# A decoder's self-attention on one NeuronCore: the value products move from the end of each step to its middle

## What is computed

```
x = LN(x + attention0(x))          causal, 16 heads of 16, rotary
x = LN(x + cross_attention(x, ctx))
x = LN(x + routed experts(x))
x = LN(x + attention1(x))          differential: 16 heads x 2 halves of 8, not causal
x = LN(x + latent attention(ctx, x))
x = LN(x + experts that choose tokens(x))

# attention0
scores = einsum('bhqd,bhkd->bhqk', q, k) * scale
scores = where(causal, finfo.min, scores)
attn = softmax(scores);  out = einsum('bhqk,bhkd->bhqd', attn, v)

# attention1
attn1 = softmax(q1 k1^T * scale) v12;  attn2 = softmax(q2 k2^T * scale) v12
a = rms(attn1 - lam * attn2) * rms_weight * (1 - LAMBDA_INIT)
```

## Time and profile before

| | |
|---|---|
| median of 3 runs | 4248.61 us (4227.96 to 4248.86) |
| the profiled execution's own time | 4232.43 us |
| its span, first to last instruction | 4230.7 us |
| PE / DVE / ACT / POOL busy | 3516.9 / 2917.2 / 1941.1 / 766.1 us |
| granted TensorE clock, mean | 0.894 of full |

### The profile page before, as it was taken

One profiled execution on the slowest core, in us unless ns is written; L12 is line 12 of the kernel. 1 busy time (PEld: TensorE's weight loads), 2 busy tenths in 40 slices (PEclk: granted clock), 3 DMA queues, 4 the chain that ended last, 5 costly groups with the idle time before them and its releaser, 6 DMA issues. The chain is left out here.

```text
span 4230.7 us, 63916 instructions
## 1 busy us (share of the span) xinstructions
PE 3516.9 (83%) x19000; PEld 1700.2 (40%) x19000; DVE 2917.2 (69%) x4353; ACT 1941.1 (46%) x3763; POOL 766.1 (18%) x1063
## 2 busy tenths in 40 slices
PE   7599999766478885999999999999965769999758
PEld 4244444433234352333333333333333435554625
DVE  6557676346546687988888888888745457776374
ACT  2156666222111032777777777777741213334121
POOL 3222223123300051000000000000022434445000
PEclk9669999788789996999999999999987879999678
DMA  5311121000010061000000000000000231110202
GB/s 196 112 36 47 46 46 31 18 35 10 0 41 15 20 198 38 23 19 17 20 22 17 21 21 17 23 19 17 10 3 29 88 123 42 28 36 1 88 17 71
DMA packets 81131, 175.80 MB, mean 42 GB/s; under 512 B 21592, under 2 KB 39008, under 8 KB 79424
## 3 DMA queue, kind: packets, MB, share of 16 engines
q1 hardware_dynamic: 79968, 165.76, 12.9%
q10 hardware_dynamic: 864, 6.29, 0.4%
HBM read 87.76 MB, written 54.72 MB: 34 GB/s over the span
## 5 line engine op out<-in xcount | busy, mean ns | idle before, releaser
L631 DVE TENSOR_REDUCE L_attn_tops<-L_attn_psM 128x2 f32<-128x1024 f32 (+3 forms) x1408 | 1560.9, 1148 | 337.3 <-PE L_attn_psM L741 329.2
L568 ACT ACTIVATE L_attn_E<-L_attn_psS 128x512 f32<-128x512 f32 (+3 forms) x2816 | 1389.3, 575 | 583.4 <-PE L_attn_psS L700 580.0
L700 PE MATMUL L_attn_psS<-L_attn_Q,L_attn_K 64*128 64x512 f32 (+3 forms) x2816 | 995.5, 437 | 108.0 <-ACT L_attn_E L568 40.1
L741 PE MATMUL L_attn_psM<-L_attn_K,L_attn_Q 62*128 62x512 f32 (+3 forms) x2816 | 1023.6, 484 | 57.1 <-DMA L_attn_K<-parts_k 30.0
L700 PEld LDWEIGHTS L_attn_psS<-L_attn_Q,L_attn_K 64*128 64x128 f32 x2816 | 474.4, 192 | 806.1 <-ACT L_attn_E L568 634.1
L716 PE MATMUL L_attn_psO<-L_attn_E,L_attn_V 128*32 128x512 f32 (+3 forms) x5632 | 738.6, 598 | 0.0
L741 PEld LDWEIGHTS L_attn_psM<-L_attn_K,L_attn_Q 62*128 62x128 f32 x2816 | 433.9, 195 | 170.4 <-DVE L_attn_tops L631 53.0
L526 POOL TENSOR_TENSOR L_AO<-L_attn_o 128x128 f32 (+1 forms) x64 | 29.4, 459 | 1463.2 <-DVE L_attn_o L664 1463.2
L1436 PE MATMUL m_psE<-m_we,m_xT 128*128 128x512 f32 x512 | 235.1, 619 | 0.0
L535 POOL TENSOR_SCALAR_AFFINE_SELECT L_attn_E<-L_attn_E 128x128 f32<-128x128 f32 x512 | 146.6, 293 | 458.6 <-ACT L_attn_E L568 447.4
L2134 ACT ACTIVATE x_E<-x_psS 128x512 f32<-128x512 f32 x256 | 138.9, 595 | 175.3 <-PE x_psS L2257 158.0
(11 more groups left out here) (339 smaller groups left out, 3787.7 us busy)
## 6 DMA issues: line engine op xcount, KB each, us to landing
parts_q<-L_proj_parts SPq DMA_DIRECT2D x64, 256.0 KB
parts_k<-L_proj_parts SPq DMA_DIRECT2D x64, 256.0 KB
L_attn_Q<-parts_q SPq DMA_DIRECT2D x192, 64.0 KB
L_attn_K<-parts_k SPq DMA_DIRECT2D x192, 64.0 KB
L_attn_Q<-parts_q SPq DMA_DIRECT2D x64, 128.0 KB
L_attn_K<-parts_k SPq DMA_DIRECT2D x64, 128.0 KB
queries<-x1p_qo SPq DMA_DIRECT2D x16, 512.0 KB
keys<-x1p_ko SPq DMA_DIRECT2D x16, 512.0 KB
```

The lines of the kernel that those rows point to most:

```text
L568: act.activation(E[(4 * n + s) % 8][:, c0:], psS[bank][:, c0:], ACT.Exp, scale=scale).then_inc(e_done, 1)
L631: dve.tensor_reduce(dst, src, AX, ALU.max).then_inc(m_read, 1)
L700: pe.matmul(psS[bank][:, c0:], K[g.slot][r:r + RH, c, kt * P:(kt + 1) * P], Q[g.slot][r:r + RH, c, q * HALF + c0:(q + 1) * HALF], start=Tr ...
L741: last = pe.matmul(psM[bank][:, j * HALF:j * HALF + n], Q[t.slot][r:r + TOP, c, qt * P:(qt + 1) * P], K[t.slot][r:r + TOP, c, h * HALF:h * ...
```

## The change

The lines that issue the value products move up within the slot. Before, they stood behind all four pairs of score and maximum matmuls; now they stand ahead of the third pair (s = 2). What each product computes, and what it waits for, is the same text.

```diff
                         for s in range(4):
+                            if s == 2 and live and step >= 1:
+                                product(g, step - 1, s_item(t, place)[0] + 3)
+                            if s == 2 and old and k == 0:
+                                product(t + -2, NS - 1, s_item(t, s_place(LATE - 1, 3, last, old))[0] + 4)
                             if live:
                                 score(t, g, step, s, place)
                             if new:
                                 most(t, 2 * n + s // 2, 1 - s % 2, at)
                         if last and n == 0:
                             turn_maxima(t, 4 if old else 0)
-                        if live and step >= 1:
-                            product(g, step - 1, s_item(t, place)[0] + 3)
-                        if old and k == 0:
-                            product(t + -2, NS - 1, s_item(t, s_place(LATE - 1, 3, last, old))[0] + 4)
                         if old and n == BACK1:
                             turn_back(t, t + -2, 1, at["back1"])
```

## The result

The changed kernel takes 4411.38 us (median of 4 runs, 4394.66 to 4425.98); the kernel before took 4241.05 on the same chip (4 runs, 4227.96 to 4248.86). The ratio is 1.041, with a 95% interval of 1.0381 to 1.0439: slower by 170 us. Forecast were 4400, with 4310 to 4480 around it. The profiled execution took 4412.34 us, its span 4410.6, and its mean granted clock was 0.892 (before: span 4230.7, 0.894).

A forecast was written before the change was run, and what follows sets the result against it. A ring of waits between PE's scores and products and the exponentials was taken to bound the kernel, no engine being full. 4232.4 + 76 (attention1) + 85 (attention0) = 4393 us, stated as 4400, range 4310 to 4480.

The forecast's parts named there:

- The steady slot: Attention1's plain slots: products now wait for the last exponential of the slot before; 2.68 us, 0.07 more than 2.61.
- the old ring: Attention1 before: exponential to score 3, products, next score 0, its exponential; links sum to 2.60 us, the slot.
- The copy of psO: Attention1, twice per group: products wait for ACT's copy of psO and start at 3.15 us, not 2.68.
- The turn back: Attention1, twice per group: maximum matmul behind score 0 waits for DVE's second reduction; slot 3.83 us for 3.19.
- The sum of a turn: Attention1: all slots of a turn make 46.6 us for 43.8, +2.7, over 32 groups +88.
- The 12 us deducted for loop ends: Attention1: at some 11 loop ends the turn back's 1.1 us wait lies under an existing stop: -12, leaving +76.
- Attention0: Slots lengthened by POOL's cut, masks, copies and turn backs: 5.9 us a group, 95 for 16, less loop ends: +85.
- The sum: Whole kernel: profiled 4232.4 + 76 + 85 = 4393 us; stated as 4400, no other stage touched.
- the low end: Whole kernel, 4310 us rounded: the turn back's wait may be absent, -45 us in each attention.
- Only the steady ring moves: Rival: copies, turn backs and POOL stay hidden; 0.07 x 512 = +36 us, 4268; chance 0.07.
- The clock falls: Rival: PE's brief stops lower the granted clock, a fifth of 704 slots slow; +124 us on top, 4517; chance 0.07.
- Faster: Rival: ACT is fed ahead during products, closing its 0.55 us idle in attention1; 4104 or 4176 us; chance 0.05.

The follow-up runs named there:

- lag2: Changed kernel with twelve buffers for exponentials instead of eight, and mid-slot products being those of two steps before: 4409.3 us, ratio 1.0423.
- copyearly: Changed kernel with ACT's copy of psO between the slot's second and third exponential instead of behind the fourth: 4346.1 us, ratio 1.0256.
- backmid: Changed kernel with the turn back moved from behind the fourth pair to directly behind the products, ahead of the third pair: 4403.9 us, ratio 1.0386.
- att0_only: Kernel before with the products moved ahead of the third pair in attention0 only: 4326.4 us, ratio 1.0201.
- nocut: Changed kernel without POOL's cut of the exponentials on the diagonal, products waiting for ACT only: 4455.6 us, ratio 1.0522.
- both: Changed kernel with psO's copy between the second and third exponential and the turn back directly behind the products: 4343.0 us, ratio 1.0252.
- nocut_early: Changed kernel without POOL's cut and with ACT's copy of psO between the second and third exponential: 4388.7 us, ratio 1.0363.
- old_backmid: Kernel before, products left at the slot's end, with its turn back moved ahead of the third pair: 4312.7 us, ratio 1.0161.

## Why the prediction was right, step by step

**The steady slot** was right: 2.67 for 2.68, and lag2 shows that it is the wait for the last exponential that costs the 0.06. One sign was off: the scores' waits grew beside the products' and did not move to them. And where the prediction says that the products wait for nothing in the old ring, the weight loads' row of 104.1 us stood in the trace; 2.60 us of links that sum to the slot without it, and products that start 1.6 us after the last exponential that they need, bear the prediction out.

**The copy of psO** was 3.23 for 3.15: after ACT's copy PE started 0.13 later and not 0.05. Over 64 such slots that is 5 us. copyearly takes 0.95 us a turn away by moving the copy alone.

**The turn back** was 3.73 to 3.75 for 3.83; the wait of line 741 on line 631 is there, and backmid shows it by taking part of it away. The 3.19 put down for the slot of before was 3.43 measured from products to products; the sum doesn't rest on it, since it takes the old turn whole, from the earlier trace rows.

**The sum of a turn** came out right, 46.7 for 46.6, though one slot wasn't in it: once a turn products are 2.95 apart where 2.68 was put down, because score 0 of k = 0 waits for the maxima's DMAs (the view names no releaser for it; in the turn from 2118.54 the last of the eight DMAs is issued at 2127.44 and the score starts at 2129.34, with its bank long free). It made up for the turn backs, which had been put too high. By the distances of products before and after, the loss of 2.9 a turn is 10 x 0.06 = 0.6 for the steady slots, 2 x 0.53 for the copies (3.23 for 2.70), 0.3 for one turn back (3.74 for 3.43), 0.7 for the other with turn_maxima behind it (3.73 + 3.10 for 3.55 + 2.62), and 0.3 for the slot of the DMAs (2.95 for 2.61). That last one the prediction did not have.

**The 12 us deducted for loop ends** in attention1 was the mis-sized term. Three turns with a loop end in them exceed three undisturbed ones by about 4.4 us before and 4.7 after, so the stop covers nothing of the new waits; and there are 9 such ends, not 11. Without the deduction the step gives 88, and 2.9 x 32 = 93 is what the turns show; 92 was measured, for the 76 forecast.

**Attention0** was forecast at +85 and was +82. The lengths of the narrow products, put down by a slope, were 0.78, 0.57 and 0.36 as worked out. The products' distances, in the order of the slots' products, were 3.18, 3.79, 2.30, 2.87, 3.01, 4.48, 3.65, 3.51, 3.17, 2.74, 2.41 and 2.99 for k = 1 to 11 and 0, against 3.34, 4.0, 2.33, 2.95, 3.09, 4.6, 3.53, 3.54, 3.13, 2.73, 2.36 and 2.95 forecast. The turn's 5.6 us over 16 groups would be 90; the stretch holds 44 us above its undisturbed turns before and 36 after, which is loop ends and clock, so the 82 is right in part by luck: the slow turns of the two kernels lie in different places and happen to cost about the same. The distances fit the prediction's links, but no run takes the whole ring out of attention0: the early copy (0.7), the moved turn back (1.2), lag2 (1.8) and the missing cut (0.9) each take a part of the 5.6 us.

**The sum.** 4393 was worked out for the profiled execution, which took 4412: 16 us more in attention1, 3 less in attention0, and 6 outside them, where none had been put down. The 4400 stated was nearer because it went by the median of the runs. The range took less than its own terms gave: the low end leaves out the 35 us that the prediction had just worked out for an earlier start.

**The rivals.** "Only the steady ring moves" is excluded by the copy and turn back slots. "Faster" is excluded: exponential 2 does wait for its score, with ACT idle 0.60 ahead of it. "The clock falls" did not come true as an effect of the change, 0.88 for 0.89 in attention0 and 0.98 in attention1. But the forecast had no place for what it stands on, that attention0's clock differs between versions of the kernel; att0_only at 0.89 and nocut at 0.76 show what such a step can bring: with 0.95 (copyearly) some 30 us less than the mechanisms give, with 0.76 (nocut) some 60 more. The rule of the Trainium skill (TensorE: Matmul & The Clock Gate, "A second HAM failure mode: psum-queue depth-cycling") that short idles between groups of matmuls can make the clock swing is not borne out by attention1, where PE's weight loads stood idle ahead of exponentials 995 + 467 times in some 512 slots, for 871 + 406 times before, and the clock kept 0.98. In attention0 the clock does swing, but not in step with the idles: nocut, without the waits for POOL, has the lowest.

What stays open is the cause of the clock's falls in attention0, and with it some tens of us of the totals of copyearly, both, lag2, nocut, nocut_early and old_backmid; and what orders attention0's masked slots without POOL.

## What to carry to other kernels

Before moving work in an in-order queue, list the rings that pass through it, for each buffer that is handed back and forth, and for each ring its links; price the moved work in every ring that it newly enters, those of another engine's buffers too. Here the new place cost 0.06 us in the steady slot, which a first look finds, and 0.3 to 0.7 at each of five rare slots: two where a single-buffered result is copied out, two where an extra user takes a bank, and one that waits for DMAs. In attention1 these made 2.3 of the 2.9 us lost in a turn. What stands behind the moved work matters as much as what it waits for: one maximum matmul behind the products instead of ahead of them was worth 0.4 us a slot. And a total can hide a mechanism: where the clock differs between versions, compare undisturbed turns at full clock before you judge an edit.

## What the runs showed of the hardware that was not expected

The granted clock of attention0 fell, for whole turns, to 0.6, and its mean lay between 0.76 and 0.95 in kernels that are one short edit away from the changed one with its 0.88 (copyearly 0.95, nocut 0.76). The same turn took 37 us at 1.00 and 48 at 0.63. By the clock alone nocut's stretch is 60 us above what its turns promise (693 for 647 - 14). A wait of PE costs hardly anything beyond the wait: products start 0.05 us after the last exponential's end and 0.13 after the copy's, and the next score comes 0.99 to 1.00 behind them whether they had waited or not.
